# Graph network kernel, front part: counts transposed on TensorE, degrees by ScalarE's square root, top nodes by two merges and a ranking, last scatters moved into the dense pass

## What is computed

```
score = X @ p / norm(p)
top_vals, top_idx = top_k(score, 128)
X_tilde = X[top_idx] * tanh(top_vals)[:, None]
W = gru_step(X_tilde, W0, ...)                      # the 128x128 weight of layer 0
deg = 1 + segment_sum(edge_weight, dst)             # per node
dinv = rsqrt(deg);  out = segment_sum(dinv[src]*w*dinv[dst] * (X @ W)[src], dst) + ...
cnt = segment_sum(1, dst)                           # edges per node, for layer 1
```

## Time and profile before

| | us |
|---|---|
| median of 3 runs | 3927.42 |
| lowest, highest | 3923.71, 3927.47 |
| profiled execution | 3923.91 |
| its span | 3922.2 |
| prelude, up to the dense pass's first transfer | 375.69 |
| dense pass, up to the edge pass's first instruction | 1472.41 |

### The profile page before, as it was taken

The page is one execution under the profiler, slowest core; times in us unless marked ns, Lnnn a source line. Parts: engine busy times, 40 slices in busy tenths (PEclk is TensorE's granted clock), DMA queues, the critical chain, the costliest instruction groups (busy, mean ns, idle before and its releaser), DMA issues. The chain is left out here.

```text
span 3922.2 us, 55046 instructions
## 1 busy us (share of the span) xinstructions
PE 3144.1 (80%) x11677; PEld 2053.1 (52%) x11677; DVE 2971.8 (76%) x7760; ACT 2315.5 (59%) x5112; POOL 2668.5 (68%) x2681
## 2 busy tenths in 40 slices
PE   5401799999999976888879999978888888678776
PEld 3200455555555544555549999974444444344443
DVE  3694899999999965777758999968999999433332
ACT  3200799999999974555533343336888888433333
POOL 4775799988889867777734444435666666477776
PEclk8755899999999997888879999999999999788887
DMA  7200333333333323444432223232222222233322
GB/s 238 77 2 7 103 125 130 123 132 121 130 124 127 128 87 112 124 130 130 126 78 86 87 89 92 87 79 62 79 78 78 78 78 78 51 87 86 83 79 56
DMA packets 250729, 377.44 MB, mean 96 GB/s; under 512 B 66186, under 2 KB 102755, under 8 KB 250649
## 3 DMA queue, kind: packets, MB, share of 16 engines
q1 hardware_dynamic: 186240, 275.69, 21.5%
q0 software_dynamic: 51328, 75.23, 8.7%
q10 hardware_dynamic: 13081, 25.69, 2.0%
HBM read 209.35 MB, written 171.27 MB: 97 GB/s over the span
## 5 line engine op out<-in xcount | busy, mean ns | idle before, releaser
L206 POOL TENSOR_TENSOR dn_rstd<-dn_var,w_minus_half 128x4 f32<-128x4 f32 x300 | 306.5, 1025 | 86.3 <-DVE dn_var L191 86.3
L1402 POOL DMA_INDIRECT p_src<-table_x,e_src x200 | 218.3, 1091 | 100.9 <-issue 54.4
L1402 POOL DMA_INDIRECT m_src<-table_x,e_src_first x200 | 194.5, 972 | 75.1 <-issue 47.2
L1223 PEld LDWEIGHTS d_pair<-w_gru_both,d_xT 128*128 128x128 f32 x800 | 196.6, 327 | 92.7 <-ACT d_xT L1261 90.5
L2194 POOL DMA_INDIRECT out_rows<-m_x,e_out_first x200 | 201.2, 1006 | 63.7 <-issue 59.7
L1402 POOL DMA_INDIRECT a_src<-table_x,e_src x200 | 200.0, 1000 | 61.2 <-issue 50.4
L612 POOL DMA_INDIRECT scratch_node_row<-o_own,e_out x200 | 196.2, 981 | 64.2 <-issue 63.3
L1223 PE MATMUL d_pair<-w_gru_both,d_xT 128*128 128x256 f32 x800 | 230.2, 432 | 11.8 <-ACT d_xT L1261 9.1
L1402 POOL DMA_INDIRECT g_own<-in_x,e_dst x200 | 188.7, 944 | 70.6 <-issue 66.7
L1402 POOL DMA_INDIRECT g_src<-in_x,e_src x200 | 188.9, 945 | 69.8 <-issue 59.7
L1676 POOL TENSOR_TENSOR pn_rstd<-pn_var,w_minus_half 128x4 f32<-128x4 f32 x50 | 52.1, 1042 | 262.1 <-DVE pn_var L191 262.1
(11 more groups left out here) (456 smaller groups left out, 10356.6 us busy)
## 6 DMA issues: line engine op xcount, KB each, us to landing
table_x<-d_x SPq DMA_DIRECT2D x300, 256.0 KB, 2.1
d_x<-in_x SPq DMA_DIRECT2D x99, 256.0 KB, 2.7
out_rows<-d_x SPq DMA_DIRECT2D x97, 256.0 KB
s_x<-in_x ACTq DMA_DIRECT2D x31, 768.0 KB, 5.8
table_x<-g_x SPq DMA_DIRECT2D x50, 256.0 KB, 2.8
scratch_post<-g_post SPq DMA_DIRECT2D x50, 256.0 KB, 2.1
p_rc<-scratch_rcount SPq DMA_DIRECT2D x50, 256.0 KB, 3.3
p_post<-scratch_post SPq DMA_DIRECT2D x50, 256.0 KB, 2.7
```

What stands on the lines that cost most here:

```text
L206: pool.tensor_tensor(self.rstd[s][:], self.var[s][:], minus_half[:], ALU.pow).then_inc(self.rooted[s], 1)
L1223: mm = pe.matmul(pair[s][:, 2 * t * P:2 * (t + 1) * P], xT[s][:, t:GROUP:TPG], W.gru_both[:], start=True, stop=True, skip_group_check=True)
L1402: pool.indirect_dma_start(out=self.rows[s][:, t * P:(t + 1) * P], out_offset=None, in_=self.table, in_offset=bass.IndirectOffsetOnAxis(ap= ...
```

## The change

Counts: TensorE transposes them from VectorE's rows into PSUM after round 3 of the scoring loop, and the trip through DRAM goes. Degrees: ScalarE takes a square root before round 5, and VectorE a reciprocal and one Newton step; GpSimd's power goes. Weight loads now stand behind the store of `t_base`, and the load of p is first on SyncE's queue. Top nodes: after the first level there are two merges (to 32 and to 8 lists, both 512 wide); only values travel to the next level, places follow behind; the 8 x 128 values that are left are compared each with all, the ranks are turned into 0/1 matrices, and eight products pick values and positions. Scatters: there are 196 instead of 200 (no empty group), 150 before the lookup chain, 8 behind it, and 38 in the dense pass's FIND slots ahead of the fetches; of the 196 fetches the last are issued in fours after `do_rstd` of groups 90 and up. The reciprocal of `e_amp` moves to the end of VectorE's prelude.

```diff
-        self.FOUND = self.EG * TPG
+        self.FOUND = groups * TPG
+        self.EARLY, self.MIDDLE = 150, 8
+        self.REST = self.FOUND - self.EARLY - self.MIDDLE
...
-        for t in range(plan.FOUND):
-            pool.indirect_dma_start(
-                out=D["node_row"], out_offset=bass.IndirectOffsetOnAxis(ap=Ed.out[:, t:t + 1], axis=0),
-                in_=self.own[:, t, :], in_offset=None, bounds_check=plan.N - 1, oob_is_err=False,
-            ).then_inc(moved, 16)
-        pool.wait_ge(moved, 16 * plan.FOUND)
...
+        self.moved = mem.sem("o_moved")
+
+    def scatter(self, pool, D, Ed, plan, t):
+
+        pool.indirect_dma_start(
+            out=D["node_row"], out_offset=bass.IndirectOffsetOnAxis(ap=Ed.out[:, t:t + 1], axis=0),
+            in_=self.own[:, t, :], in_offset=None, bounds_check=plan.N - 1, oob_is_err=False,
+        ).then_inc(self.moved, 16)
+
+    def settled(self, pool, plan):
+        pool.wait_ge(self.moved, 16 * plan.FOUND)
...
-        sp.dma_start(D["count"], part[0][:]).then_inc(stored, 16)
-        sp.dma_start(D["wsum"], part[1][:]).then_inc(stored, 16)
         sp.dma_start(D["rcount"], inv[:]).then_inc(stored, 16)
-        sp.wait_ge(stored, 80)
+        sp.wait_ge(stored, 48)
...
+    def tensor_counts(pe):
+
+        for k in range(2):
+            pe.wait_ge(counted, k + 1)
+            for t in range(TPG):
+                mm = pe.transpose(tokens[:, (k * TPG + t) * EG:(k * TPG + t + 1) * EG], part[k][:, t:GROUP:TPG],
+                                  W.ident[0:EG, 0:EG])
+        mm.then_inc(turned_counts, 1)
...
-    def sync_counts(sp):
...
-        sp.dma_start(flat(cnt[:]), tok(D["count"])).then_inc(loaded, 16)
-        sp.dma_start(flat(Own.deg[:]), tok(D["wsum"])).then_inc(loaded, 16)
...
+        count, weight = counts(dve)
+        dve.tensor_scalar(flat(deg[:]), weight, 1.0, None, ALU.add).then_inc(degs, 1)
+        then(dve.tensor_copy(flat(cnt[:]), count))
+        dve.wait_ge(tables, 4)
+        then(dve.scalar_tensor_tensor(Own.own[:, :, 2], Own.own[:, :, 0], 1.0, cnt[:], ALU.add, ALU.subtract))
...
+        dve.wait_ge(rooted, 1)
+        then(dve.reciprocal(Ed.dinv[:], Ed.dinv[:]))
+        then(dve.tensor_tensor(square[:], Ed.dinv[:], Ed.dinv[:], ALU.mult))
+        then(dve.scalar_tensor_tensor(square[:], square[:], -0.5, deg[:], ALU.mult, ALU.mult))
+        then(dve.scalar_tensor_tensor(Ed.dinv[:], square[:], 1.5, Ed.dinv[:], ALU.add, ALU.mult))
+        dve.tensor_copy(Own.own[:, :, 1], Ed.dinv[:]).then_inc(tabled, 1)
...
+    def scalar_root(act):
+        act.wait_ge(degs, 1)
+        act.activation(Ed.dinv[:], deg[:], ACT.Sqrt).then_inc(rooted, 1)
+
     def scalar(act):
-        act.wait_ge(loaded, 16 * LOADS)
+        act.wait_ge(tabled, 1)
         act.activation(Ed.amp[:], cnt[:], ACT.Ln, bias=1.0).then_inc(logged, 1)
...
-    LEVELS = 3
+    LEVELS, LISTS = 2, 8
...
-    ROWS = (32, 4, 1)
+    ROWS = (32, LISTS)
...
+        for n, (r, values, places) in enumerate(((P, v1, n1i), (ROWS[0], vm[0], fmi[0]), (ROWS[1], None, fmi[1]))):
+            if values is not None:
+                sp.wait_ge(value_found, n + 1)
+                sp.dma_start(row(D[f"top_val{n}"], r), values[:]).then_inc(values_stored, 16)
+                sp.wait_ge(values_stored, 16 * (n + 1))
+                sp.dma_start(merged[n][:], row(D[f"top_val{n}"], ROWS[n])).then_inc(lists_loaded, 16)
+            sp.wait_ge(place_found, n + 1)
+            sp.dma_start(row(D[f"top_id{n}"], r), places[:]).then_inc(places_stored, 16)
+        sp.wait_ge(places_stored, 16 * (LEVELS + 1))
...
+        pool.wait_ge(named, 1)
+        pool.wait_ge(places_stored, 16 * (LEVELS + 1))
+        for k in range(LEVELS + 1):
+            pool.indirect_dma_start(out=ids[:, k + 1:k + 2], out_offset=None, in_=D[f"top_id{LEVELS - k}"],
                                     in_offset=bass.IndirectOffsetOnAxis(ap=ids[:, k:k + 1], axis=0)).then_inc(found, 16)
...
+    def gpsimd_found(pool):
+        pool.wait_ge(found, 16 * (LEVELS + 2))
...
+        pe.wait_ge(value_found, 2 + 1)
+        pe.transpose(pt[:, 0:LISTS], vm[1][:], W.ident[0:LISTS, 0:LISTS]).then_inc(columned, 1)
+        for half, rows in enumerate((prz, pin)):
+            pe.wait_ge(spreaded, half + 1)
+            for c in range(LISTS // 2):
+                mm = pe.transpose(rows[:, c * TOP:(c + 1) * TOP], spread[:, half * LISTS // 2 + c, :], W.ident[:])
+            mm.then_inc(broadcast, 1)
+        for c in range(LISTS):
+            pe.wait_ge(membered, 1)
+            mm = pe.matmul(phn[:, 0:2], member[:, c, :], pair[:, c, :], start=c == 0, stop=c == LISTS - 1)
+        mm.then_inc(picked, 1)
         pe.wait_ge(loaded, 16 * 7)
+        pe.wait_ge(named, 1)
...
+            last = TOP // 8 - 1
             for r in range(TOP // 8):
                 c = slice(8 * r, 8 * r + 8)
                 then(dve.max(out[:, c], values[:]))
+                if r == last:
+                    dve.sem_inc(value_found, 1)
                 then(dve.max_index(place[:, c], out[:, c], values[:]))
-                then(dve.match_replace(values[:], out[:, c], values[:], LOW))
+                if r < last:
+                    then(dve.match_replace(values[:], out[:, c], values[:], LOW))
...
             best(merged[n], vm[n], im[n])
-            then(dve.tensor_copy(fm[n][:], im[n][:]))
-            then(dve.tensor_scalar(fm[n][:], fm[n][:], basef[0:r, n + 1:n + 2], None, ALU.add))
-            dve.tensor_copy(fmi[n][:], fm[n][:]).then_inc(best_found, 1)
+            if n == 0:
+                numbered(fmi[n], im[n], fm[n], basef[0:r, n + 1:n + 2])
+        dve.wait_ge(columned, 1)
+        then(dve.tensor_copy(pair[:, :, 0], pt[:, 0:LISTS]))
+        for half in range(2):
+            part = slice(half * LISTS // 2, (half + 1) * LISTS // 2)
+            dve.tensor_copy(spread[:, part, :], pair[:, part, 0:1].to_broadcast([P, LISTS // 2, TOP])).then_inc(spreaded, 1)
+        numbered(fmi[1], im[1], fm[1], basef[0:LISTS, 2:3])
...
+        for c in range(LISTS):
+            v = pair[:, c, 0:1]
+            near, far = (prz, pin) if c < half else (pin, prz)
...
+                then(dve.tensor_scalar(above[:, 0:here * TOP], near[:, 0:here * TOP], v, 0.0, ALU.is_ge, ALU.add,
+                                       accum_out=before[:, c:c + 1]))
+            if here < half - 1:
+                then(dve.tensor_scalar(above[:, 0:(half - 1 - here) * TOP], near[:, (here + 1) * TOP:half * TOP], v, 0.0,
+                                       ALU.is_gt, ALU.add, accum_out=after[:, c:c + 1]))
+            then(dve.tensor_scalar(above[:, 0:half * TOP], far[:, 0:half * TOP], v, 0.0,
+                                   ALU.is_gt if c < half else ALU.is_ge, ALU.add, accum_out=rank[:, c:c + 1]))
...
+        dve.tensor_tensor(member[:], counting[:].unsqueeze(1).to_broadcast([P, LISTS, TOP]), over(rank[:], TOP),
+                          ALU.is_equal).then_inc(membered, 1)
+        dve.wait_ge(picked, 1)
+        then(dve.tensor_copy(val[:], phn[:, 0:1]))
+        dve.tensor_copy(ids[:, 0:1], phn[:, 1:2]).then_inc(named, 1)
...
         @block.sync
         def _(sp):
+            marks["sync"](sp)
             rows["sync"](sp)
-            marks["sync"](sp)
             tables["sync"](sp)
+            tables["sync_base"](sp)
             fold["sync"](sp)
             rows["sync_store"](sp)
-            tables["sync_counts"](sp)
             top["sync"](sp)
             top["sync_merge"](sp)
 
         @block.gpsimd
         def _(pool):
+            tables["gpsimd"](pool)
             fold["gpsimd"](pool)
-            tables["gpsimd"](pool)
             top["gpsimd"](pool)
             tables["done"](pool)
-            Own.root(mem, pool, Ed)
-            Own.scatter(mem, pool, D, Ed, plan)
+            for t in range(plan.EARLY):
+                Own.scatter(pool, D, Ed, plan, t)
             top["gpsimd_find"](pool)
+            for t in range(plan.EARLY, plan.EARLY + plan.MIDDLE):
+                Own.scatter(pool, D, Ed, plan, t)
+            top["gpsimd_found"](pool)
 
...
             rows["vector"](dve)
             tables["vector"](dve)
+            rows["vector_last"](dve)
+            tables["vector_first"](dve)
             fold["vector"](dve)
+            top["vector"](dve)
             tables["vector_scalers"](dve)
-            top["vector"](dve)
...
             for j in range(Q):
-                if j == 4:
-                    tables["scalar"](act)
+                if j == 5:
+                    tables["scalar_root"](act)
                 marks["copy"](act, j)
             marks["move"](act)
+            tables["scalar"](act)
...
+            turn = [-plan.REST]
+
+            def find():
+                n = turn[0]
+                turn[0] += 1
+                if n < 0:
+                    Own.scatter(pool, D, Ed, plan, plan.FOUND + n)
+                if n == 0:
+                    Own.settled(pool, plan)
```

(13 more changed lines are left out.)

174 lines of the change are left out of this document (94 added, 80 removed).

## The result

| | before | after |
|---|---|---|
| median | 3925.57 us (3923.08 to 3927.47, 4 runs) | 3869.76 us (3868.5 to 3872.75, 4 runs) |
| span of the profiled execution | 3922.2 | 3866.8 |

What follows compares the result with a forecast made beforehand. Bound by a prelude that is a chain of single engines, then a full dense pass. Terms -20.6 - 56.8 - 23.2 + 1.4 + 32.5 = -66.7 us gave 3861 us, within 3846 to 3874, range 3824 to 3886.

Steps and rivals of the forecast that it cites:

- Term 1: Counts and degrees, up to the first selection: no wait for counts, earlier scatters and weight folding; -20.6 us (-23 to -12).
- I take 40: Weights' arrival in the front: VectorE starts folding at 40 us, from 38 to 48, which is 19.3 us earlier than 59.31.
- I give 1.1 us for that: TensorE's folding blocks: allowance of 1.1 us for a low clock after some 8 us of idling before them.
- Term 2: Selection, from its start to the ids: narrower levels and a ranking take 133.9 us instead of 190.7; -56.8 us (-63 to -46).
- Term 3: Lookup chain: scatters end at about 230, so the wait from ids to first lookup falls from 23.38 to 0.2; -23.2 us.
- Term 4: Front's end: the reciprocal of `e_amp`, moved to VectorE's end where nothing covers it; +1.4 us.
- Eight scatters behind it take 10.3 us: Behind the lookup chain: GpSimd's eight scatters run beside a GRU step of VectorE and TensorE that is as long.
- Term 5: Dense pass: 34 surplus fetches in fours ahead of `dl_rstd` delay the last steps and drain; +32.5 us (10 to 44).
- A: Drain of the dense pass: idle time takes most fetches, the fetch cost is 10 us or less, total 3838; 20%.
- B: Front gains less: weights arrive at 48 instead of 40 and comparisons cost double, 8 + 10 us, total 3879; 14%.
- C: Scoring loop: the change's root doesn't free ScalarE before round 5, losing 20 us of the front's gain, total 3881; 3%.
- D: Front: scatters stretched by VectorE make GpSimd the bound again; at 2.37 us each the kernel takes 3995, slower; 3%.

Runs made afterwards that it cites:

- runs 5 and 6: Changed kernel, with the `t_base` store behind the weight loads (4331.10 us), or ScalarE's x loads after the first six held until weights land (4311.96 us); kernel before about 4428.
- Run 2: Changed kernel with TensorE's folding blocks behind round 14 of the scoring loop instead of 10, later fold steps four rounds later: 3861.09 us, ratio 0.9837.
- run 1: Changed kernel with all 158 front scatters ahead of the lookup chain and none behind it, instead of 150 and 8: 3865.59 us, one run.
- run 3: Changed kernel with 28 of the 34 surplus fetches behind `dl_rstd` instead of ahead of it, in the same drain steps: 3855.61 us, ratio 0.9823.
- run 4: Changed kernel with no scatters in the dense pass, 188 ahead of the lookup chain and 8 behind it: 3861.49 us, ratio 0.9844.

## Why the prediction was right, step by step

The waits that the prediction named are the ones that went, and the price that it named for the drain was paid. The total owes something to a wide range and to chance: the front is 13.0 us longer than predicted (289.5, not 276.5) and the dense pass is 1.2 us longer; 2.9 us of that came back in edge passes whose instructions nobody changed.

- **Term 1 was mis-sized: -10.9 instead of -20.6, and outside its own range of -23 to -12.** The mechanism stood: no wait for counts, TensorE idle ahead of VectorE, a low clock behind the idle time. The failed step is "I take 40" for VectorE's fold: it was 47.34, within the stated 38 to 48, and 12.0 us earlier than before instead of 19.3. The text named the reasons, the store of `t_base` and more of x; runs 5 and 6 measured them: 2.8 to 3.5 us for the store, and at least 8.2 us for x with the store still ahead (VectorE, not a weight, set that start). The second step that failed is "I give 1.1 us for that", the low clock. The wait that TensorE no longer costs came as forecast: from VectorE's start to TensorE's second folding block it is 11.8 us (47.34 to 59.14) and was 14.1 (59.31 to 73.42), 2.3 us less, with 2.37 credited. But the clock was still low in the blocks themselves, not only behind them: their last 24 matmuls cost 7.14 us instead of 5.08, and round 11's transposes 2.73 instead of 1.53, so 3.3 us instead of 1.1. With 12.0, 2.3 and 3.3 the term is -11.0. Run 2, where TensorE does rounds of the scoring loop in place of that wait, has the 24 at 5.09 us.
- **Term 2: -56.8 predicted, -56.1 measured.** Up to the last level's last value it is 112.2 us (predicted 112.3). The comparisons came within 0.2 us of a sum worked out from fixed cost and cost an element of other operations; the products took 0.8 us more than the 2.8 given for them. Each sum is read out by an instruction of its own of 0.08 us.
- **Term 3: exact.** The scatters ended at 232.5 (predicted 230), 1.31 us apart. The time to spare was 31.8 us instead of 24 because the ids came 10.4 us late.
- **Term 4: +1.4 predicted, +4.0 measured.** The reciprocal cost what was said. The 2.4 us that no step held are GpSimd's scatters at the block's end (run 1). "Eight scatters behind it take 10.3 us, beside VectorE's and TensorE's GRU step, which is as long" counted their issue alone, and not the 5.26 us between the last of them and the block's end.
- **Term 5: +32.5 predicted, +33.7 measured.** Position was the cause of 16 us of it (run 3). The steps of groups 90 and 91, 8.9 us, cost the same on either side (8.7 in run 3), so there it is the amount of GpSimd's work that counts. In the next step 2.3 us are lost with no surplus fetch as well, at a lower granted clock (run 4). What makes up the rest was not taken apart. That groups 97 and 98 cost 0.6 was wrong by 1.2.
- **Rivals.** A, the drain takes the fetches for nothing, is out: 1130.4 us against 1097. B held in its first half, the weights at 47.3 (it had 48, against 40); the comparisons did not cost double. C is out: ScalarE's root stood between two copies. D is out: beside VectorE's folding the scatters' median was 978 ns, the longest of them 1718.

## What to carry to other kernels

Work that is put into "free" time of an engine in a drain should stand behind the instruction that other engines wait for, not ahead of it: the same 28 fetches cost 16 us more on the wrong side of one root. In steps that are full already it doesn't matter where it stands (4.3 and 4.4 us, against 4.4 and 4.5). When a stall goes, write down what each later start waits for, the transfers above all: x, which had paused in the old stall, now delayed the weights, and the next gain was in letting another engine run past a wait. And count a program block's end as a stage with its own last instruction on every engine.
